# Shifted-window attention rows on one Trainium2 core: residual adds, exponentials, first key tile, residual staging and value transfers take new places in the engines' orders

## What is computed

```
x = x + outlook_attention(group_norm(x))     # 3x3 neighbourhood weights, softmax over 9, 6 heads
x = x + window_attention(group_norm(x))      # 7x7 windows, rolled by 3, 12 heads of 16
window_attention: q, k, v = xw @ Wqkv.T + b            (xw: one window's 49 tokens)
                  p = softmax(q*hd**-0.5 @ k.T + rel_bias + shift_mask)   # 49 x 49 per head
                  out = (p @ v) @ Wproj.T + bproj
```

## Time and profile before

| | |
|---|---|
| median of 3 runs | 3873.07 us (3870.67 to 3879.84) |
| the profiled execution: its time, its span | 3867.02 us, 3865.2 us |
| busy share of the span | TensorE matmul 88%, VectorE 70%, GpSimd 59%, ScalarE 48% |
| mean granted TensorE clock | 0.928 of full speed |

### The profile page before, as it was taken

How to read it: one execution, slowest core, us unless ns; L and a number is a source line. 1 busy time by engine, 2 the same in 40 slices (tenths; PEclk the granted TensorE clock), 3 DMA queues, 4 the chain that set the end, 5 groups by cost and what they waited for, 6 DMA issues and landing times.

```text
span 3865.2 us, 105389 instructions
## 1 busy us (share of the span) xinstructions
PE 3398.0 (88%) x39908; PEld 2047.9 (53%) x39908; DVE 2706.8 (70%) x4465; ACT 1874.1 (48%) x3602; POOL 2293.2 (59%) x1889
## 2 busy tenths in 40 slices
PE   6988889888898888988889888898889988899888
PEld 3456644566445664455644566445663466634655
DVE  5966669666795667956678567786668766687665
ACT  3444544555435544355543555445554455544555
POOL 3765547665475654756547655566555666466664
PEclk7999989999998989999999999999989999899898
DMA  4722237221461223612246112561215512164121
GB/s 106 143 63 63 70 70 140 58 79 56 89 136 41 80 61 86 133 52 69 72 92 130 52 55 73 103 123 49 73 54 121 111 44 79 53 131 97 53 68 59
DMA packets 204343, 317.51 MB, mean 82 GB/s; under 512 B 16922, under 2 KB 176154, under 8 KB 203802
## 3 DMA queue, kind: packets, MB, share of 16 engines
q0 software_dynamic: 31936, 148.66, 19.7%
q1 hardware_dynamic: 171866, 161.61, 14.2%
HBM read 45.97 MB, written 38.54 MB: 22 GB/s over the span
## 4 chain that ended last, share of the span: by engine, by line
PE 49%; ACT 12%; issue 11%; DMA 11%; DVE 11%; POOL 3%; SPq 2%; DVEq 0%; ACTq 0%; POOLq 0%
PE P L699 7%; DMA prod<-prod 6%; PE P L731 6%; DMA vbd<-vs 5%; PE P L695 3%; PE P L654 3%; PE P L488 3%; PE P L656 3%; PE P L754 3%; DVE sp__70 L1531 3%; ACT pt L1129 3%; ACT sp__70 L1121 3%; PE P L718 2%; ACT kbd L1104 2%; ACT kbd L1103 2%
## 5 line engine op out<-in xcount | busy, mean ns | idle before, releaser
L1783 POOL TENSOR_TENSOR sp__70<-sp__70,rc 128x588 f32<-128x588 f32 x512 | 589.9, 1173 | 829.6 <-DVE rc L1548 829.6
L1427 DVE TENSOR_TENSOR prod<-P,vpad 128x896 f32<-128x896 f32 (+1 forms) x768 | 791.2, 1050 | 131.0 <-PE P L488 120.1
L1545 DVE TENSOR_REDUCE sm<-sp__70 128x12 f32<-128x588 f32 x512 | 377.9, 738 | 710.0 <-ACT sp__70 L1121 706.0
L1776 POOL TENSOR_TENSOR sp__70<-sp__70,mx 128x588 f32<-128x588 f32 x512 | 598.3, 1173 | 165.6 <-DVE mx L1538 158.0
L488 PE MATMUL P<-at,sel 108*128 108x448 bf16 x1512 | 426.5, 361 | 61.3 <-DVE prod L1427 30.9
L1531 DVE TENSOR_TENSOR sp__70<-P,relb 128x588 f32<-128x588 f32 x512 | 383.8, 750 | 88.4 <-PE P L718 88.4
L1129 ACT ACTIVATE pt<-P 98x588 f32<-98x588 f32 x512 | 313.3, 659 | 233.9 <-PE P L731 227.8
L1696 POOL DMA_DIRECT2D prod<-prod x216 | 202.3, 941 | 358.6 <-DVE prod L1427 355.1
L731 PEld LDWEIGHTS P<-ident,sp__70 113*98 113x98 f32 x3072 | 357.1, 141 | 94.9 <-issue 34.9
L731 PE MATMUL P<-ident,sp__70 113*98 113x113 f32 x3072 | 384.9, 281 | 25.0 <-DVE sp__70 L1531 24.0
L1538 DVE TENSOR_REDUCE mx<-sp__70 128x12 f32<-128x588 f32 x512 | 389.5, 761 | 9.3
(11 more groups left out here) (256 smaller groups left out, 7308.9 us busy)
## 6 DMA issues: line engine op xcount, KB each, us to landing
prod<-prod POOLq DMA_DIRECT2D x216, 672.0 KB, 5.5
vbd<-vs SPq DMA_DIRECT2D x512, 147.0 KB
xin<-in_x SPq DMA_DIRECT2D x126, 336.0 KB, 4.1
out<-ot SPq DMA_DIRECT2D x184, 168.0 KB, 4.0
out<-ot SPq DMA_DIRECT2D x80, 84.0 KB
wn<-in_L_conv_qkv_weight SPq DMA_DIRECT2D x2, 432.0 KB, 6.3
wno<-in_L_conv_proj_weight SPq DMA_DIRECT2D x2, 144.0 KB, 7.4
self<-in_sel SPq DMA_DIRECT2D x3, 91.1 KB
```

The source lines that it names most:

```text
L1427: tt(by_row(dst), by_row(P[:, b:b + len(op), 0:CT]), val, ALU.mult).then_inc(prod_ok, 1)
L1545: red(sm[:, b, :], sp_[:, b, :].rearrange("p (h k) -> p h k", h=NH), AX.X, ALU.add).then_inc(p_sum, 1)
L1776: tt(per_head(sp_[:, b, :]), per_head(sp_[:, b, :]), spread(mx[:, b, :]), ALU.subtract).then_inc(t_sub, 1)
L1783: tt(per_head(sp_[:, b, :]), per_head(sp_[:, b, :]), spread(rc[:, b, :]), ALU.mult).then_inc(p_norm, 1)
```

## The change

- SyncE starts spread(w+1, 0) and spread(w+1, 1) before it waits for x_turned and loads the input chunk.
- ScalarE takes exp_step of half m = 0 out of its place after keep_probs. It stands now at the end of the step before, after late: step p ends with the exponential of pair p+2, half 0. One call ahead of row 0 starts the sequence, and last_row is reordered to match.
- VectorE copies the first key tile (R0) of rows 2 to 7 out of PSUM (first_keys_kept, two tensor_scalar operations) in step 1, between the two prob_sums. ScalarE's keep_keys of that tile goes; the second tile's counts two, and TensorE waits for k_first as well.
- VectorE does all three finish calls in step 2, between the two prob_sums, and the wrap copy in step 3, between the two prob_sums. The three stat_x calls are done together in step 0, between the two prob_sums.
- GpSimd does its staging operation between the two shift_steps.

```diff
@@ sync
+                    if w < NW - 1:
+                        spread(w + 1, 0)
+                        spread(w + 1, 1)
                     if 1 <= w and w + 1 < CHUNKS:
                         sp.wait_ge(x_turned, ONE + T * (CHUNKS * (i + 1) + w))
                         load(w + 1)
-                    if w < NW - 1:
-                        spread(w + 1, 0)
-                        spread(w + 1, 1)
@@ tensor: scores
                         pe.wait_ge(k_kept, ONE + T * (NW * i + w + 1))
+                        if w > 1:
+                            pe.wait_ge(k_first, ONE + (NW - 2) * i + w - 1)
@@ tensor: after, p == 1
                         pe.wait_ge(k_kept, ONE + T * (R + 1) + 2)
+                        pe.wait_ge(k_first, ONE + (NW - 2) * i + w)
                         begin_out(w - 1, freed=(k_kept, ONE + T * (R + 2)))
@@ scalar: keep_keys
-                       ).then_inc(k_kept, 1)
+                       ).then_inc(k_kept, 2 if w > 1 and n == 1 else 1)
@@ scalar: early
-                    elif p == 1:
-                        keep_keys(w + 1, 0, ROW_BANKS[0])
@@ scalar: window_row
                         w1, p1 = pair_after(w, p, 1)
-                        exp_step(w1, p1, 0)
                         exp_step(w1, p1, 1)
                         late(w, p)
+                        w2, p2 = pair_after(w, p, 2)
+                        exp_step(w2, p2, 0)
@@ scalar: last_row
                     keep_probs(w, 0, 1)
+                    exp_step(w, 1, 1)
                     keep_next(w, 0, Y_BANK)
                     keep_next(w, 1, R0)
-                    exp_step(w, 1, 0)
                     keep_next(w, 2, R1)
-                    exp_step(w, 1, 1)
+                    exp_step(w, 2, 0)
 
                     keep_probs(w, 1, 0)
                     keep_probs(w, 1, 1)
-                    exp_step(w, 2, 0)
                     exp_step(w, 2, 1)
@@ scalar: ahead of row 0
                     keep_queries(0, n, bank, EDGE)
+                exp_step(0, 1, 0)
                 for m in range(2):
                     keep_window_values(0, 1, m, (R0, R1)[m])
@@ vector
+                def first_keys_kept(w):
+
+                    dve.wait_ge(k_mm, ONE + T * (NW * i + w) + 1)
+                    for e in range(2):
+                        last = ts(kbd[:, w % 2, 0, e, :], P[:, R0, 0:RT], me[:, e:e + 1], kb[:, 0, e:e + 1],
+                                  ALU.mult, ALU.add)
+                    last.then_inc(k_first, 1)
@@ vector: finish loses its last part, which becomes wrap_out
-                    if n == T - 1:
-                        dve.wait_ge(fin_ok, ONE + T * (R + 1))
-                        wrap = lambda c: fin[:, :, c:c + RT].rearrange("p j (r n) -> p j r n", n=W)[:, :, :, 0:SHIFT]
-                        nc.vector.tensor_copy(wrap(0), wrap(W)).then_inc(fin_wrap, 1)
+                def wrap_out(w):
+                    dve.wait_ge(fin_ok, ONE + T * (NW * i + w + 1))
+                    wrap = lambda c: fin[:, :, c:c + RT].rearrange("p j (r n) -> p j r n", n=W)[:, :, :, 0:SHIFT]
+                    nc.vector.tensor_copy(wrap(0), wrap(W)).then_inc(fin_wrap, 1)
@@ vector: window_row
-                        if w >= 1 and p == 2:
-                            finish(w - 1, 0, ROW_BANKS[0])
-                            finish(w - 1, 1, ROW_BANKS[1])
+                        prob_sum(w1, p1, 0)
+                        if w >= 1 and p == 1:
+                            first_keys_kept(w + 1)
+                        elif w >= 1 and p == 2:
+                            for n in range(T):
+                                finish(w - 1, n, ROW_BANKS[n])
                         elif w >= 1 and p == 3:
-                            finish(w - 1, 2, ROW_BANKS[2])
+                            wrap_out(w - 1)
                         elif w >= 2 and p == 0:
-                            stat_x(i + 1, w - 2, (0, 1))
-                        elif w >= 2:
-                            stat_x(i + 1, w - 2, (2,))
-                        prob_sum(w1, p1, 0)
+                            stat_x(i + 1, w - 2, range(T))
                         prob_sum(w1, p1, 1)
@@ gpsimd: window_row
                         if w1 < NW:
                             shift_step(w1, p1, 0)
-                            shift_step(w1, p1, 1)
                         if p == 0 and 0 < w < NW - 1:
                             stage_residual(w, 2)
...
                         if w1 < NW:
+                            shift_step(w1, p1, 1)
                             normalize_step(w1, p1, 0)
                             normalize_step(w1, p1, 1)
```

More of the change, by code:

```diff
@@ L197, in mixer @@
         xw_first = sem("xw_first"); xw_ok = sem("xw_ok"); xr_ok = sem("xr_ok"); vs_zero = sem("vs_zero"); stage_due = sem("stage_due")
-        q_mm = sem("q_mm"); q_kept = sem("q_kept"); k_mm = sem("k_mm"); k_kept = sem("k_kept")
+        q_mm = sem("q_mm"); q_kept = sem("q_kept"); k_mm = sem("k_mm"); k_kept = sem("k_kept"); k_first = sem("k_first")
         vv_mm = sem("vv_mm"); vs_kept = sem("vs_kept"); v_in = [sem("v_in0"), sem("v_in1")]
@@ L209, in mixer @@
                    padd_ok, o_mm, x1_kept, x1_stat, x1_wrap, xw_first, xw_ok, xr_ok, vs_zero, q_mm, q_kept,
-                   k_mm, k_kept, vv_mm, vs_kept, *v_in, sc_mm, t_add, t_max, t_sub, p_exp, p_sum, p_rec,
+                   k_mm, k_kept, k_first, vv_mm, vs_kept, *v_in, sc_mm, t_add, t_max, t_sub, p_exp, p_sum, p_rec,
                    p_norm, p_turned, p_kept, y_mm, y_kept, out_mm, fin_ok, fin_wrap, ot_mm, ot_kept, *out_in]
@@ L1631, in last_row @@
                     finish(w, 2, R2)
+                    wrap_out(w)
                 score_bias(0, 0, 0)
```

## The result

| | before | after |
|---|---|---|
| median | 3871.87 us (4 runs) | 3553.49 us (4 runs, 3543.87 to 3556.17) |
| ratio to before, 95% interval | 1 | 0.9172 (0.9148 to 0.9197) |
| profiled execution: time, span | 3867.02, 3865.2 us | 3556.17, 3554.1 us |
| mean granted clock | 0.928 | 0.957 |

What follows compares the result with a forecast made beforehand. TensorE, the engine with least idle time, was taken as the bound. 334 us gone less 31 us of new waits gave net 303 off 3867: 3564, set at 3570 us because the profiled execution lay 6 below the median; range 3530 to 3660.

Steps and rivals of the forecast that it cites:

- The third finish: Step 2: window_values no longer waits for this late VectorE operation; 157.4 us gone over 48 rows.
- the clock: TensorE's value products and transposes behind step 2's wait return to full rate: 101 us gone, bounds 67 to 134.
- the walk: Timing of one row from measured durations; claimed TensorE has no gap over 0.6 us left.
- The value transfer: Step 0: its DMAs start ahead of the input load, so TensorE's wait goes; 33.2 us.
- The first key tile: Step 1: ScalarE loses two copies, keep_out and remaining key copies come 1.2 us earlier; 42.3 us gone.
- The added wait of ScalarE: Step ends wait for GpSimd's shift: free in steps 0 to 2; step 3 costs 24 us, plus 5 for keep_next.
- Row 7: Step 0: keep_out calls behind the exponential delay scores 0.3 us, about 2 us in all; the rest hidden.
- The loop through GpSimd: Rival: the ScalarE-GpSimd loop binds, adding 0.5 us in three steps per row, 72 us: 3642; chance 0.17.
- the clock came back: Answers the rival that TensorE's clock stays low, without the 101 us: 3671; chance 0.08.
- the third finish is in time: Answers the rival that step 2's third finish is late all the same: 3829; chance 0.04.
- rival 4: ScalarE's wait at the step's end puts everything in series, 10 to 48 us more: about 3900; chance 0.05.
- The wrap copy: Step 3: could hold GpSimd 0.2 us per row, 10 us in all if on the path; counted as 0.

Runs made afterwards that it cites:

- third_finish_back: Changed kernel with only the third finish moved back to the start of step 3: 3784.11 us, 0.9744.
- exps_alone: Kernel before with only the half-0 exponential moved to the end of the step before: 3844.67 us, 0.9914.
- first_keys_back: Changed kernel with the first key tile copied by ScalarE ahead of keep_probs in step 1 again, none on VectorE: 3560.81 us, 0.9184.
- exps_and_finishes: Kernel before with the new places of the half-0 exponential and of the finishes, nothing else: 3602.89 us, 0.9308.
- finish_after_max: Changed kernel with the third finish moved behind the first score_max of ahead in step 2: 3608.40 us, 0.9314.
- finishes_alone: Kernel before with only the three finishes in step 2 between the sums and the wrap copy in step 3: 3723.00 us, 0.9603.
- finish_after_bias: Changed kernel with the third finish moved behind the second score_bias of ahead in step 2: 3706.52 us, 0.9572.

## Why the prediction was right, point by point

- **The third finish, 157 us, and the clock, 101 us.** Right, in mechanism and size. Steps 2 and 3 became shorter by 5.06 + 0.38 us in rows 2 to 6 and 3.68 + 0.35 in row 1, 250 us; of the forecast that is 157 + 101 - 24 - 5 = 229. The clock's share was taken from one row and halved for half of the rows. In the kernel before, products and transposes take 1.5 to 3.1 us more than at full rate in every one of the 48 rows, 111 us together; third_finish_back puts 83 us on the clock by its time, within the bounds 67 to 134. "TensorE has no gap over 0.6 us left in the walk" held in rows 2 to 6, but for single gaps, not in row 1, where the gap in attend reaches 1.33 us; the walk did not cover it.
- **The value transfer, 33 us.** Right: step 0 shortened by 37 us in the 48 rows, and undoing it costs 39.
- **The first key tile, 42 us.** The step that failed is "keep_out and the remaining key copies come some 1.2 us earlier and step 1's 20.7 + 12.3 + 9.3 = 42.3 us go". Step 1 gave 0.57 x 40 + 0.79 x 8 = 29 us, and most of it came from the exponential that left ScalarE's order, not from the key tile: exps_alone has 7.44 us without the tile's move, and first_keys_back is 12 us slower in its steps and not measurably in its time. In row 1 it is the other way round: there exps_alone has 7.35 us, first_keys_back 7.34 and the changed kernel 6.60. In TensorE's waits, the 20.7 us went with the exponential, and of the 21.6 us for key copies 13.9 are left, 0.34 us in each of rows 2 to 6. What was overlooked is the transpose that keep_out waits for.
- **Two tensor_scalar from PSUM, 481 to 560 ns.** Outside the bounds: 672 ns each, by the group of the kernel after:

```profile
L1530 DVE TENSOR_SCALAR kbd<-P,me,kb 128x392 f32<-128x392 f32 x96 | 60.5, 672 | 0.4 <-PE P L656 0.4
```

The cover (the second half's exponential) was long enough all the same.
- **The added wait of ScalarE.** Right that it is free in steps 0, 1 and 2 and costs in step 3, where the chain is as written. The exponential, the value copies and keep_probs of step 3 (turn_probs at 357.36), in ScalarE's timeline:

```profile
357.30 0.70 ACT L1124 ACTIVATE sp__70<-sp__70 128x588 f32<-128x588 f32 x1 [3.07 <-POOL sp__70 L1789]
357.90 0.97 ACT L1117 ACTIVATE vs<-P 98x192 f32<-98x192 f32 x4
358.74 1.23 ACT L1132 ACTIVATE pt<-P 98x588 f32<-98x588 f32 x2
```

The exponential ends at T3 + 0.64 (forecast 0.55), the value copies at 1.5 (1.7), and TensorE waits 0.24 us (0.5): 9.5 us instead of 24.
- **Only implicit in the forecast: the parts need each other.** The prediction used "half 0's exponential is ready at about 0.6" under the finishes, but never said what the finishes would bring without it. exps_and_finishes shows that 81 us hang on the pair, and undoing the exponential's move costs 168 us with everything else in place, where alone it brought 33.
- **Row 7.** 2 us were forecast as a loss. Its keep_out calls do stand behind the exponential, and scores wait for keep_next; TensorE's timeline of the changed kernel, pass 1:

```profile
894.32 0.99 PE L382 MATMUL P<-ident,xin 112*128 112x112 f32 x8 [0.24 <-ACT ot L1139]
896.96 0.89 PE L720 MATMUL P<-kbd,qs 32*64 32x98 f32 x48 [1.65 <-ACT xa L967]
```

That wait is 1.65 us, not 0.3, and comes in each of the eight passes (13.2 us). Step 0 lasts 9.31 us against 7.89, so the forecast that the rest of the step hides it failed; but step 1 lasts 8.87 against 10.84, and the first three steps gain 0.7 us. The prediction had nothing for step 1 of this row; that its small figure for the row did no harm is luck.
- **The sum.** 303 us forecast, 311 in the spans, 318 in the medians. The terms miss in both directions: the new waits of step 3 were sized too high (24 us against 9.5), the clock too low (101 against 111), step 1 too high (42 against 29), so part of the agreement is luck. Two sums of the prediction are off without changing the forecast: with clock 134 and new waits 10 the lower bound is 3516, not 3527, and the loop with staging and value copies in step 3 adds up to 7.9 us, not 7.4.
- **The rivals.** The loop through GpSimd did not bind, the clock came back, the third finish is in time, and the series of rival 4 did not form. Steps of 7.3, 7.1, 7.3 and 8.9 us were forecast for a full row; 7.23, 7.44, 7.20 and 8.73 were measured.
- **The wrap copy.** By the Trainium skill (SBUF — State Buffer, SBUF: two separate sides) it could have held GpSimd 0.2 us per row. Its line in the kernel after (min/median/max ns):

```profile
L1579 DVE COPY fin<-fin x64: 157/169/279, 297.1 to 3548.0; 128x63 f32<-128x63 f32 x64
```

Before it was 202/800/803. Two other runs have it in other places, finish_after_max and finishes_alone:

```profile
L1579 DVE COPY fin<-fin x64: 202/461/466, 297.3 to 3607.9; 128x63 f32<-128x63 f32 x64
...
L1569 DVE COPY fin<-fin x64: 137/139/204, 302.0 to 3718.2; 128x63 f32<-128x63 f32 x64
```

In these two kernels, the one before and the changed one, the copies and GpSimd's operations were laid side by side in the rows between 300 and 440 us and between 740 and 860 us. Where a shift of GpSimd runs beside the copy, the copy ends some 0.05 us after the shift, wherever it began: in the kernel before the shift ends at 409.94 and the copy, begun at 409.20, at 410.00; in finish_after_max at 805.78 and 805.84 (begun at 805.38); in the changed kernel at 359.09 and 359.14 (begun at 358.97). In finishes_alone no operation of GpSimd runs beside it, and it takes 0.14 us. So the copy waits for the shift, as the rule says, and in its new place it is mostly clear of it. GpSimd was not held noticeably, and the forecast's zero stands.

## What to carry to other kernels

Look at what an engine does between the moment its input is ready and the moment it delivers to the engine that bounds the kernel: a 0.56 us addition, queued behind nine other instructions after its input was ready, cost nearly 5 us per row (third_finish_back), as wait and as lower clock behind it. Before such a piece is moved forward, ask what it now stands in front of; here it stood in front of work that TensorE needs, and this was hidden only once another engine's operation (the exponential) was moved a whole step ahead: each move alone brought 154 and 33 us, both brought 268. When an engine is relieved of work, follow its next wait: the time that ScalarE was freed of in step 1 went into waits for transposes, until a copy was put into one of the gaps.

## What was not expected of the hardware

- TensorE's clock after short waits: after 1.33 to 1.39 us idle it stayed up in 39 of 46 rows and fell in 7 (finish_after_max); after 2.0 to 2.1 us it fell in 40 of 43 (finish_after_bias); after 3.1 to 3.3 us it fell in all 48 rows of the kernel before. The length of the gap alone does not decide: gaps of 1.33 us in row 1 of the changed kernel did one and the other. The last 0.7 us of wait were the dear ones, 100 us.
- VectorE's tensor_scalar of 128 x 392 float32 takes 672 ns from PSUM, against 481 ns from SBUF, and more than the 555 ns of the addition that reads the same width from PSUM and SBUF.
- A VectorE copy of 128 x 63 float32 within SBUF took 0.14 us with GpSimd idle and up to 0.80 us beside a GpSimd subtraction; it ended some 0.05 us after that subtraction.
